# The half-filled sixth tile of the feed-forward: its down product in two passes, with the low part of the activations beside the high part

## The chip, the cores and the metric

The kernel runs on one NeuronCore of a Trainium2 chip. The metric is the device time of one execution in microseconds, as the median of several runs. A profiled execution has a time of its own, and a span from its first to its last instruction.

## What is computed

Eight sequences of 512 tokens with 256 features pass through two layers. Layer 0 is a rotating recurrence with short convolutions and a gated normalisation, then a mixture of experts. Layer 1 is causal attention with 16 heads of 128, then a feed-forward whose weights are looked up in a table of 16 values. All arithmetic of the reference is float32. What matters here is the last block:

```python
def _L1_ffn_ref(x, lut, gate_idx, up_idx, down_idx):   # INTER = 688, HIDDEN = 256
    def _ghost_linear(x, idx, lut):
        w = lut[idx]
        return jnp.einsum('bsh,oh->bso', x, w)
    gate = _ghost_linear(x, gate_idx, lut)
    up = _ghost_linear(x, up_idx, lut)
    h = jax.nn.silu(gate) * up
    return _ghost_linear(h, down_idx, lut)
...
x = x + _L1_ffn_ref(_layernorm(x, axis=-1), L1_ffn_lut, L1_ffn_gate_idx, L1_ffn_up_idx, L1_ffn_down_idx)
```

## The kernel before

**Products in three passes.** Where the reference multiplies float32 matrices, the kernel splits each operand into a high part (the value copied to FP32R, by ScalarE, `high` at L647) and a low part (the value less its high part, by VectorE, `low` at L1055). `mm3` (L1621 to L1623) adds up three matmuls: high times high, high times low, low times high. In the down product the first operand, which sits in the array, is the activation and the second, which streams, is the weight. So L1621 is activation high by weight high, L1622 activation high by weight low, L1623 activation low by weight high. The profile names the two operands of a matmul the other way about: `bank<-fw_high,fa_high` is L1621.

**The feed-forward.** The 688 inner features are laid out in NM = 6 tiles of 128 partitions. Five are full (NFULL = 5). The sixth, m = 5, holds 48 features, padded to 64. Its gate and up rows share one product (`rest`): gate in bank rows 0 to 63, up in rows 64 to 127. ScalarE applies SiLU to the first half, VectorE multiplies it by the second half into `ft` (`ffn_product`, L1506), ScalarE copies the high part into `fa2[0]` (`high_unit`), VectorE writes the low part into `fa2[1]` (`ffn_low`, L1509). `fa2` is a pair of tiles of 128 partitions x 6 x 512 tokens. Rows 64 to 127 of m = 5 hold no features: both parts are cleared there once, ahead of the first batch's low part (two memsets, L1514), and the weights have zeros in the same rows.

**The down product.** For one batch `ffn_down` (L2010) is called for n = 0 and 1. Each call does two of the four token tiles of 128; a token tile is 6 x 3 matmuls that add up in half a PSUM bank, 128 tokens x 256 features. The last batch uses `last_down` (L2019), which goes by m and does all four token tiles for each.

**Where it stands in the order of work.** Each engine's program is written out by hand and in order. Layer 1's attention is a loop over 8 batches x 16 heads (g = 16 b + h). TensorE's share of one head (`head`, in the tensor block) is: `extra_read` and `project_out` of the head before, `make_qk` of the next, `transpose_probs`, `make_v` of the one after next, then `extra`, then `make_z`, then `scores` of the next head. `extra` holds the work of the feed-forward of the batch before: at heads 6 to 11 the gate and up products (H_UNIT = 6), at heads 13 and 14 the two `ffn_down` calls (H_DOWN = 13). The down product of batch 6 and all of batch 7's feed-forward follow behind the last head. VectorE's `head` has `score_max`, `low_q`, `low_probs`, `low_k`, then `ffn_low`, then the rest down to `low_z`; `project_out` on TensorE waits for `low_z`. At head 12 VectorE also writes the low part of the next batch's normalised input (`h_low`).

**Weights.** The host sends table indices `fidx`, which the kernel turns into weights early on; `down` is a view of 128 partitions x 6 x 256 of the weights' high and low tiles. Indices that pad are LUTN = 16, which gives zero.

**Other matmuls that are spoken of.** The output projection of layer 0 (`out_product`, L1699 and L1703, and `out_product_part`, L1716 and L1720) is in float32. For a pair of sequences it first uses 128 rows of partitions (L1699, L1716), then 64 rows, partitions 0 to 63 or 64 to 127 (L1703, L1720). `rows_product` makes layer 0's projections in three passes; of 192 rows of weights it takes 128 and then 64, as 128 and 64 columns of the array.

Of the kernel before, what the change touches and what calls it, by code (L numbers as in the profile page):

```python
# [17 lines left out]
ALU = mybir.AluOpType  # L18
ACT = mybir.ActivationFunctionType
F32 = mybir.dt.float32  # L20
# [5 lines left out]
P = 128  # L26
NB, T, D = 8, 512, 256
# [19 lines left out]
NFULL = INTER // P  # L47
REST = INTER - NFULL * P
NM = NFULL + 1
# [48 lines left out]
def two_layer_program(nc, x_in, w0, wab, cw, invf, rmsw, wo0, cent, gbias, wexp, iota16, tri, tileno, wpair, fidx, lut, out):  # L98
    ctx = ExitStack()
    with ctx:  # L100
        def sb(name, shape, dt=F32):
            return ctx.enter_context(nc.sbuf_tensor(name, shape, dt))

        def sem(name):
            return ctx.enter_context(nc.semaphore(name))
# [4 lines left out]
        bank = [ctx.enter_context(nc.psum_tensor(f"bank{i}", [P, 512], F32)) for i in range(8)]  # L110
# [76 lines left out]
        fa2 = [sb(f"fa2_{part}", [P, NM, T], F32R) for part in ("high", "low")]  # L187
# [37 lines left out]
        ft = [sb(f"ft{i}", [P, T]) for i in range(2)]  # L225
# [6 lines left out]
        def ffn_weights(part):  # L232
            w = fw2[part]
            at = [0, KD * NFULL * P, 2 * KD * NFULL * P, KD * (2 * NFULL + 1) * P, FW]
            views = [w[:, a:b] for a, b in zip(at, at[1:])]
            return [view.rearrange("p (k n) -> p k n", k=KD) for view in views[:3]] + [
                views[3].rearrange("p (m n) -> p m n", m=NM)]
# [126 lines left out]
        s_fa = sem("ffn_activation_split")  # L364
# [44 lines left out]
        def down_bank(b):  # L409
            return {LAST_BATCH: 4, LAST_BATCH - 1: 2}.get(b, 6)  # L410
# [612 lines left out]
        def _(v):  # L1023
# [27 lines left out]
            def low(parts, src, done, at=lambda part: part[:], scale=None):  # L1051

                high_ = at(parts[0]).bitcast(F32)
                if scale is None:
                    v.tensor_tensor(at(parts[1]), src, high_, ALU.subtract).then_inc(done, 1)  # L1055
                else:
                    v.scalar_tensor_tensor(at(parts[1]), src, scale, high_, ALU.mult, ALU.subtract).then_inc(done, 1)
# [450 lines left out]

            def ffn_low(b, m):  # L1509
                v.wait_ge(s_fh, b * NM + m + 1)  # L1510
                used = slice(0, P if m < NFULL else P // 2)
                if b == 0 and m == NFULL:
                    for part in fa2:
                        v.memset(part[P // 2:P, m, :].bitcast(F32), 0.0)  # L1514
                low(fa2, ft[m % 2][used, :], s_fa, lambda part: part[used, m, :])

            def ffn_add(b, n):
                v.wait_ge(s_fd, 2 * b + n + 1)
# [3 lines left out]
            def head(g):  # L1522
# [25 lines left out]
                if b > 0 and H_UNIT < h <= H_UNIT + NM:  # L1548
                    ffn_low(b - 1, h - H_UNIT - 1)
# [29 lines left out]
            for i in range(NT):  # L1579
# [4 lines left out]
                ins = v.bn_stats(stats[:, i, :], xs[0][:, i, :])  # L1584
# [20 lines left out]
            for m in range(NM):  # L1605
                if m + 1 < NM:
                    ffn_product(last, m + 1)
                ffn_low(last, m)
# [4 lines left out]
        def _(pe):  # L1613
            mm = pe.matmul
# [4 lines left out]
            def mm3(dst, w, x, start, stop):  # L1619

                mm(dst, w[0], x[0], start=start, stop=False)  # L1621
                mm(dst, w[0], x[1], start=False, stop=False)  # L1622
                return mm(dst, w[1], x[0], start=False, stop=stop)  # L1623

            def parts(pair, at):
                return [at(t) for t in pair]

            def project3(dst, w_at, x):

                for k in range(KD):  # L1630
                    ins = mm3(dst, [w_at(part, k) for part in range(2)], parts(x, lambda t: t[:, k, :]),
                              k == 0, k == KD - 1)
                return ins
# [362 lines left out]
            gate, up, rest, down = zip(ffn_weights(0), ffn_weights(1))  # L1996

            def ffn_unit(b, m):
# [8 lines left out]
                project3(bank[n][:], lambda part, k: gate[part][:, k, m * P:(m + 1) * P], f2).then_inc(s_fg, 1)  # L2007
                project3(bank[n + 1][:], lambda part, k: up[part][:, k, m * P:(m + 1) * P], f2).then_inc(s_fu, 1)

            def ffn_down(b, n):  # L2010
                pe.wait_ge(s_fa, (b + 1) * NM)
                for i in (2 * n, 2 * n + 1):
                    for m in range(NM):
                        ins = mm3(bank[down_bank(b) + n][:, (i % 2) * D:(i % 2 + 1) * D],
                                  parts(fa2, lambda t: t[:, m, i * P:(i + 1) * P]), [w[:, m, :] for w in down],
                                  m == 0, m == NM - 1)
                ins.then_inc(s_fd, 1)

            def last_down(m):  # L2019
                b = LAST_BATCH  # L2020
                pe.wait_ge(s_fa, b * NM + m + 1)
                for i in range(NT):
                    ins = mm3(bank[down_bank(b) + i // 2][:, (i % 2) * D:(i % 2 + 1) * D],
                              parts(fa2, lambda t: t[:, m, i * P:(i + 1) * P]), [w[:, m, :] for w in down],
                              m == 0 and i % 2 == 0, m == NM - 1 and i % 2 == 1)
                    if m == NM - 1 and i % 2 == 1:
                        ins.then_inc(s_fd, 1)

            def extra(g):
                b, h = divmod(g, NH)  # L2030
                if b > 0:
                    if h == H_TURN3:
                        pe.wait_ge(s_ob, g + START)
                        turn(3, b - 1)
                    if 0 <= h - H_UNIT < NM:
                        pe.wait_ge(s_ob, g + START)
                        ffn_unit(b - 1, h - H_UNIT)
                    if b < LAST_BATCH and 0 <= h - H_DOWN < 2:
                        pe.wait_ge(s_ob, g + START)
                        ffn_down(b - 1, h - H_DOWN)  # L2040
                if b + 1 < NB and h == H_TURN2:
                    pe.wait_ge(s_ob, g + START)
                    turn(2, b + 1)
# [40 lines left out]
            for n in range(2):  # L2084
                ffn_down(last - 1, n)
            pe.wait_ge(s_ob, NG + START)
            turn(3, last)
            for m in range(NM):
                if m >= 2:
                    pe.wait_ge(s_fm, last * NM + m - 1)  # L2090
                ffn_unit(last, m)
                if m >= 2:
                    last_down(m - 2)
            for m in (NM - 2, NM - 1):
                last_down(m)
# [76 lines left out]
```

## Time and profile before

| | us |
|---|---|
| median of three runs | 2242.14 |
| lowest, highest | 2241.34, 2242.36 |
| profiled execution, its own time | 2239.54 |
| its span, first to last instruction | 2237.8 |
| TensorE busy in the span | 2142.9 (96%) |
| VectorE busy | 1678.7 (75%) |
| ScalarE busy | 1375.3 (61%) |
| GpSimd busy | 539.9 (24%) |

PE is TensorE's matmuls, PEld its weight loads, which can run beneath matmuls; DVE is VectorE, ACT ScalarE, POOL GpSimd. Matmuls are pipelined and the end of one is modelled, so their durations overlap: what a matmul costs is the distance from its start to the next one's start. A form such as `64*128` at a matmul is rows times columns of the array in use. "issue" in place of a releaser means that the engine waited for nothing that the profile shows.

### The profile page before, as it was taken

Reading aid. Unit: us, or ns where it says so; the run is one execution under the profiler, and the core shown is the slowest. Engines: PE = TensorE matmul, PEld = TensorE weight load, DVE = VectorE, ACT = ScalarE, POOL = GpSimd, SP = SyncE. Lnnn points to the kernel's source line nnn. Section 1 sums busy time; section 2 is a strip of 40 time slices with the busy share of each in tenths; the row PEclk is TensorE's granted clock in tenths of the full one; section 3 lists DMA queues with packets and bytes.
Section 4 is the critical chain, followed back from the end, with each engine's and each line's share of the span. In section 5 each row is a group of like instructions: output and inputs, shape, how many; then the busy total and the mean of one; then the engine's idle time right before and its main releaser. Section 6 shows DMA issues by size and latency. Waiting matters only on the chain. (4 is left out here: it accounts for less than half of the span.)

```text
span 2237.8 us, 37588 instructions
## 1 busy us (share of the span) xinstructions
PE 2142.9 (96%) x13012; PEld 1862.8 (83%) x13012; DVE 1678.7 (75%) x4385; ACT 1375.3 (61%) x3554; POOL 539.9 (24%) x522
## 2 busy tenths in 40 slices
PE   6899999869999999999999999999999999999998
PEld 5677777747788899889989998998898899899887
DVE  7888897888875777876866777677677768767664
ACT  4443433125636766785786678578677757866772
POOL 0212323420113323222321321231141222122220
PEclk9999999999999999999999999999999999999999
DMA  8001000236531112111211211121121121111100
GB/s 293 1 1 53 24 34 24 101 136 206 174 118 38 62 53 67 57 43 62 67 43 39 89 44 39 62 71 39 39 90 43 39 81 53 38 44 61 39 20 20
DMA packets 88555, 145.81 MB, mean 65 GB/s; under 512 B 8368, under 2 KB 55856, under 8 KB 88368
## 3 DMA queue, kind: packets, MB, share of 16 engines
q1 hardware_dynamic: 67904, 112.73, 15.7%
q0 software_dynamic: 6144, 16.79, 2.2%
q10 hardware_dynamic: 14320, 13.90, 1.8%
q8 instruction: 106, 1.74, 0.3%
q14 instruction: 81, 0.66, 0.1%
HBM read 105.63 MB, written 37.75 MB: 64 GB/s over the span
## 5 line engine op out<-in xcount | busy, mean ns | idle before, releaser
L602 POOL TENSOR_TENSOR wo_low<-wraw_o,wo_high 128x256 fp32r<-128x256 f32 x128 | 94.5, 739 | 1097.5 <-ACT wo_high L647 1097.5
L939 ACT ACTIVATE pr<-bank,negmax 128x128 f32<-128x128 f32 (+3 forms) x512 | 263.0, 526 | 143.7 <-DVE negmax L1465 143.7
L1055 DVE TENSOR_TENSOR p_low<-bank,p_high 128x512 fp32r<-128x512 f32 (+2 forms) x384 | 190.4, 551 | 116.0 <-ACT p_high L647 115.4
L647 ACT ACTIVATE p_high<-bank 128x512 fp32r<-128x512 f32 (+2 forms) x384 | 177.8, 497 | 150.0 <-PE bank L1967 150.0
L1465 DVE CUSTOM_DVE_ANT_0 bank<-bank,causal 128x128 f32<-128x128 f32 (+3 forms) x512 | 234.9, 521 | 1.1 <-PE bank L1623 1.1
L1492 DVE SCALAR_TENSOR_TENSOR xs<-bank,rinv,xs 128x256 f32<-128x256 f32 x512 | 211.9, 477 | 1.2 <-PE bank L1623 1.2
L1621 PE MATMUL bank<-h_high,wqk_high 128*128 128x512 f32 x512 | 203.4, 397 | 2.2 <-DVE h_low L1055 2.2
L1622 PE MATMUL bank<-h_low,wqk_high 128*128 128x512 f32 x512 | 203.4, 397 | 0.0
L1623 PE MATMUL bank<-h_high,wqk_low 128*128 128x512 f32 x512 | 203.3, 397 | 0.0
L592 POOL TENSOR_TENSOR wqk_low<-wraw,wqk_high 128x512 fp32r<-128x512 f32 x128 | 165.5, 1293 | 81.5 <-ACT wqk_high L647 81.5
L1055 DVE TENSOR_TENSOR z_low<-bank,z_high 128x512 fp32r<-128x512 f32 x128 | 88.5, 691 | 128.0 <-ACT z_high L647 127.9
L1967 PEld LDWEIGHTS bank<-ident,pr 128*128 128x128 f32 x1280 | 147.7, 140 | 18.6 <-ACT pr L939 1.4
L1967 PE MATMUL bank<-ident,pr 128*128 128x128 f32 x1280 | 160.5, 272 | 1.1 <-ACT pr L939 1.1
L1621 PE MATMUL bank<-wo_high,z_high 128*128 128x256 f32 x512 | 148.2, 289 | 9.2 <-DVE z_low L1055 6.5
L1621 PE MATMUL bank<-wv_high,h_high 128*128 128x256 f32 x512 | 154.9, 303 | 0.0
L1623 PE MATMUL bank<-wv_high,h_low 128*128 128x256 f32 x512 | 144.5, 282 | 0.0
L1622 PE MATMUL bank<-wv_low,h_high 128*128 128x256 f32 x512 | 144.3, 282 | 0.0
L1622 PE MATMUL bank<-wo_low,z_high 128*128 128x256 f32 x512 | 144.2, 282 | 0.0
L1623 PE MATMUL bank<-wo_high,z_low 128*128 128x256 f32 x512 | 144.1, 281 | 0.0
L1621 PE MATMUL bank<-k_high,q_high 128*128 128x384 f32 (+2 forms) x384 | 140.8, 367 | 0.0
L1621 PE MATMUL bank<-p_high,v_high 128*128 128x512 f32 (+2 forms) x384 | 130.8, 341 | 1.7 <-DVE p_low L1055 1.7
L647 ACT ACTIVATE z_high<-bank 128x512 fp32r<-128x512 f32 x128 | 76.4, 597 | 88.9 <-PE bank L1978 88.9
(312 smaller groups left out, 6436.1 us busy)
## 6 DMA issues: line engine op xcount, KB each, us to landing
wraw<-in_wpair SPq DMA_DIRECT2D x64, 512.0 KB, 4.1
wraw<-in_wpair SPq DMA_DIRECT2D x64, 256.0 KB, 4.3
wraw_o<-in_wpair SPq DMA_DIRECT2D x64, 256.0 KB, 2.5
tokens_by_expert<-zero SPq DMA_DIRECT2D x10, 1024.0 KB, 10.5
xt<-tokens_by_expert SPq DMA_DIRECT2D x40, 256.0 KB, 3.2
expert_results<-ey ACTq DMA_DIRECT2D x40, 256.0 KB, 3.6
wres<-in_wexp SPq DMA_DIRECT2D x1, 6144.0 KB, 20.7
xs<-x_between_stages SPq DMA_DIRECT2D x8, 512.0 KB, 4.6
```

The lines of the kernel that those rows point to most:

```text
L592: pool.tensor_tensor(low, wraw[r][:, 2 * e * D:2 * (e + 1) * D], high.bitcast(F32), ALU.subtract).then_inc(s_wq, 1)
L602: pool.tensor_tensor(wo2[e][1][:], wraw_o[r][:, e, :], wo2[e][0][:].bitcast(F32), ALU.subtract).then_inc(s_wo, 1)
L647: sc.activation(dst, src, ACT.Copy, scale=scale).then_inc(done, 1)
L939: ins = sc.activation(pr[:, i, 0:(i + 1) * P], score(i), ACT.Exp, scale=-1.0, bias=negmax[:, i:i + 1], accum_out=rsum[:, i:i + 1])
L1055: v.tensor_tensor(at(parts[1]), src, high_, ALU.subtract).then_inc(done, 1)
L1465: ins = v.tensor_tensor_reduce(score(i), score(i), causal[:, (NT - 1 - i) * P:NT * P], -1.0, -NEG, ALU.add, ALU.min, negmax[:, i:i + 1])
L1492: ins = v.scalar_tensor_tensor(xb[:, i, :], bank[6 + n][:, (i % 2) * D:(i % 2 + 1) * D], rinv[:, i:i + 1], xb[:, i, :], ALU.mult, ALU.add)
L1621: mm(dst, w[0], x[0], start=start, stop=False)
L1622: mm(dst, w[0], x[1], start=False, stop=False)
L1623: return mm(dst, w[1], x[0], start=False, stop=stop)
L1967: ins = pe.transpose(bank[2 + n][:, at:at + P], pr[:, i, j * P:(j + 1) * P], ident[:])
```

## The change

Rows 64 to 127 of the sixth tile are put to use. `ffn_low` for m = 5 writes the low part of the activations to rows 64 to 127 of the high tile `fa2[0]`, below the high part in rows 0 to 63, and the two memsets go. On the host the sixth tile of the down weights' rows is laid out twice, in rows 0 to 63 and again in rows 64 to 127. The new `down_product` keeps three matmuls for full tiles. For m = 5 it has two: all 128 rows of `fa2[0]` by the high weights, which adds high times high and low times high at once, and rows 0 to 63 of `fa2[0]` by rows 0 to 63 of the low weights. Both `ffn_down` and `last_down` use it. Waits and semaphores stay.

```diff
--- before.py
+++ after.py
@@ -1508,11 +1508,12 @@
 
             def ffn_low(b, m):
                 v.wait_ge(s_fh, b * NM + m + 1)
-                used = slice(0, P if m < NFULL else P // 2)
-                if b == 0 and m == NFULL:
-                    for part in fa2:
-                        v.memset(part[P // 2:P, m, :].bitcast(F32), 0.0)
-                low(fa2, ft[m % 2][used, :], s_fa, lambda part: part[used, m, :])
+                used = slice(0, P // 2)
+                if m < NFULL:
+                    low(fa2, ft[m % 2][:], s_fa, lambda part: part[:, m, :])
+                else:
+                    v.tensor_tensor(fa2[0][P // 2:P, m, :], ft[m % 2][used, :], fa2[0][used, m, :].bitcast(F32),
+                                    ALU.subtract).then_inc(s_fa, 1)
 
             def ffn_add(b, n):
                 v.wait_ge(s_fd, 2 * b + n + 1)
@@ -2007,22 +2008,28 @@
                 project3(bank[n][:], lambda part, k: gate[part][:, k, m * P:(m + 1) * P], f2).then_inc(s_fg, 1)
                 project3(bank[n + 1][:], lambda part, k: up[part][:, k, m * P:(m + 1) * P], f2).then_inc(s_fu, 1)
 
+            def down_product(dst, m, i, start, stop):
+                at = slice(i * P, (i + 1) * P)
+                if m < NFULL:
+                    return mm3(dst, parts(fa2, lambda t: t[:, m, at]), [w[:, m, :] for w in down], start, stop)
+                used = slice(0, P // 2)
+                mm(dst, fa2[0][:, m, at], down[0][:, m, :], start=start, stop=False)
+                return mm(dst, fa2[0][used, m, at], down[1][used, m, :], start=False, stop=stop)
+
             def ffn_down(b, n):
                 pe.wait_ge(s_fa, (b + 1) * NM)
                 for i in (2 * n, 2 * n + 1):
                     for m in range(NM):
-                        ins = mm3(bank[down_bank(b) + n][:, (i % 2) * D:(i % 2 + 1) * D],
-                                  parts(fa2, lambda t: t[:, m, i * P:(i + 1) * P]), [w[:, m, :] for w in down],
-                                  m == 0, m == NM - 1)
+                        ins = down_product(bank[down_bank(b) + n][:, (i % 2) * D:(i % 2 + 1) * D], m, i,
+                                           m == 0, m == NM - 1)
                 ins.then_inc(s_fd, 1)
 
             def last_down(m):
                 b = LAST_BATCH
                 pe.wait_ge(s_fa, b * NM + m + 1)
                 for i in range(NT):
-                    ins = mm3(bank[down_bank(b) + i // 2][:, (i % 2) * D:(i % 2 + 1) * D],
-                              parts(fa2, lambda t: t[:, m, i * P:(i + 1) * P]), [w[:, m, :] for w in down],
-                              m == 0 and i % 2 == 0, m == NM - 1 and i % 2 == 1)
+                    ins = down_product(bank[down_bank(b) + i // 2][:, (i % 2) * D:(i % 2 + 1) * D], m, i,
+                                       m == 0 and i % 2 == 0, m == NM - 1 and i % 2 == 1)
                     if m == NM - 1 and i % 2 == 1:
                         ins.then_inc(s_fd, 1)
 
@@ -2151,8 +2158,10 @@
 
     full = slice(0, NFULL * P)
     rest = np.concatenate([padded(idx[NFULL * P:], P // 2) for idx in (gi, ui)])
+    down_rest = padded(di.T[full.stop:], P // 2)
+    down_rows = np.concatenate([di.T[full], down_rest, down_rest])
     fidx = np.concatenate([kt(gi[full].T).reshape(P, -1), kt(ui[full].T).reshape(P, -1), kt(rest.T).reshape(P, -1),
-                           padded(di.T, NM * P).reshape(NM, P, D).transpose(1, 0, 2).reshape(P, -1)], 1)
+                           down_rows.reshape(NM, P, D).transpose(1, 0, 2).reshape(P, -1)], 1)
     fidx = fidx.reshape(P, NB, LC).transpose(1, 0, 2)
     lut = np.tile(a["L1_ffn_lut"], (P, 1))
 
```

## Rows read from the trace of the kernel before

**Rows 1.** The page: busy us, share, instructions; granted clock in 40 slices.

```profile
PE 2142.9 (96%) x13012; PEld 1862.8 (83%) x13012; DVE 1678.7 (75%) x4385; ACT 1375.3 (61%) x3554; POOL 539.9 (24%) x522
...
PEclk9999999999999999999999999999999999999999
```

**Rows 2.** Waits of TensorE, 890 to 2195 us: total us, times, longest.

```profile
PE bank L1621 <- DVE z_low L1055: 6.5, 8, 0.9
PE bank L1621 <- DVE p_low L1055: 1.7, 2, 0.8
PE bank L1621 <- issue: 1.5, 1, 1.5
PE bank L1967 <- ACT pr L939: 1.1, 1, 1.1
```

**Rows 3.** Groups by form, down product: count, busy us, mean ns, idle before.

```profile
L1621 PE MATMUL bank<-fw_high,fa_high 128*128 128x256 f32 x192 | 54.4, 283 | 0.6 <-DVE fa_low L1055 0.6
...
L1621 PEld LDWEIGHTS bank<-fw_high,fa_high 128*128 128x128 f32 x192 | 36.7, 191 | 0.9 <-DVE fa_low L1055 0.8
```

**Rows 4.** Timeline of PE, end of a down product: start, us, instruction.

```profile
1018.91 0.28 PE L1622 MATMUL bank<-fw_low,fa_high 128*128 128x256 f32 x1
1019.03 0.28 PE L1623 MATMUL bank<-fw_high,fa_low 128*128 128x256 f32 x1
1019.15 0.40 PE L1621 MATMUL bank<-p_high,v_high 128*128 128x512 f32 x1
```

**Rows 5.** Timeline of PE, layer 0's output projection, 359 to 364 us.

```profile
359.13 0.59 PE L1699 MATMUL bank<-wo_all,go 128*128 128x256 f32 x2
359.66 0.70 PE L1703 MATMUL bank<-wo_rest,ge 64*128 64x256 f32 x2
360.19 0.59 PE L1703 MATMUL bank<-wo_rest,go 64*128 64x256 f32 x2
...
362.78 0.59 PE L1703 MATMUL bank<-wo_rest,go 64*128 64x256 f32 x2
363.30 0.50 PE L1621 MATMUL bank<-hT_high,w_high 128*128 128x512 f32 x1
363.64 0.39 PE L1622 MATMUL bank<-hT_low,w_high 128*128 128x512 f32 x1
```

**Rows 6.** Waits of the weight loads, whole span: total us, times, longest.

```profile
PEld bank L1703 <- issue: 2.0, 6, 0.3
...
PEld bank L1720 <- issue: 1.0, 3, 0.3
```

**Rows 7.** Timeline of PE in `rows_product`, from 128 to 64 columns.

```profile
307.65 0.39 PE L1623 MATMUL bank<-hT_high,w_low 128*128 128x512 f32 x1
307.88 0.40 PE L1621 MATMUL bank<-hT_high,w_high 128*64 128x512 f32 x1
308.12 0.39 PE L1622 MATMUL bank<-hT_low,w_high 128*64 128x512 f32 x1
```

**Rows 8.** Timeline of all engines, batch 1, head 12, 1001 to 1008.5 us.

```profile
1002.71 0.69 DVE L1055 TENSOR_TENSOR k_low<-bank,k_high 128x512 fp32r<-128x512 f32 x1
...
1003.56 0.48 DVE L1514 MEMSET fa_high<- 64x512 f32 x1 [0.16 <-issue]
1004.11 0.48 DVE L1514 MEMSET fa_low<- 64x512 f32 x1
...
1008.01 0.36 PE L1621 MATMUL bank<-wo_high,z_high 128*128 128x256 f32 x1 [0.87 <-DVE z_low L1055]
```

**Rows 9.** Timeline of all engines, batch 2, head 12, 1196.5 to 1202 us.

```profile
1196.72 0.69 DVE L1055 TENSOR_TENSOR k_low<-bank,k_high 128x512 fp32r<-128x512 f32 x1
...
1201.12 0.35 PE L1621 MATMUL bank<-wo_high,z_high 128*128 128x256 f32 x1
```

**Rows 10.** Groups by form on DVE, sixth tile: product and subtraction.

```profile
L1506 DVE TENSOR_TENSOR ft<-fsg,bank 64x512 f32<-64x512 f32 x8 | 5.5, 690 | 16.7 <-ACT fsg L959 16.7
...
L1055 DVE TENSOR_TENSOR fa_low<-ft,fa_high 64x512 fp32r<-64x512 f32 x8 | 5.4, 676 | 0.1
```

## Prediction

> **What bounds the kernel now.** I read the page first. TensorE is busy for 2142.9 of 2237.8 us and its granted clock stands at nine tenths or more in every slice [rows 1]. Busy alone proves little, since matmuls overlap, so next come the waits of TensorE in the stretch where the feed-forward runs inside the heads, 890 to 2195 us: 6.5 + 1.7 + 1.5 + 1.1 = 10.8 us of waiting in 1305 us [rows 2]. Nothing else holds TensorE there. Any array time added or taken in a head is therefore a change of the span, with no slack of another engine to swallow it. Third, the groups by form: the down product is 192 matmuls at each of its three lines, 576 in all [rows 3] (the other two lines have the same count). A sixth of them, 96, belong to tile m = 5.
>
> The mean of 283 ns in that group is no price. The timeline gives it: successive down matmuls start at 1018.91, 1019.03 and 1019.15, so one costs 0.12 us of the engine's time [rows 4], and the work behind the product, the first of make_z, follows at the same step without a gap.
>
> **The matmuls removed.** For each of 8 batches and 4 token tiles, tile m = 5 goes from three matmuls to two: 32 fewer, 32 x 0.12 = 3.84 us less [rows 4]. The first remaining pass keeps its shape (128 rows). The second has 64 rows and as many columns. How long does a 64-row matmul take? The output projection of layer 0 has some: between 360.19 and 362.78 six pairs of 64-row matmuls go by, 2.59 us for twelve, 0.216 us each, and such a pair lasts 0.59 us like the pair of 128 rows at 359.13, which has as many columns [rows 5]. Half the rows save nothing in time, so the second pass is taken at the full 0.12 us. Bounds: 0.06 if halving the rows halved the time, for which no row speaks, and 0.12.
>
> **The changes of shape that are added.** This is the part that decides. Now every matmul of the down product has 128 rows. Afterwards each token tile of each batch goes 128 rows to 64 and back to 128 rows. The same crossing stands in the trace [rows 5]:
> - In: the last 128-row matmul starts at 359.13 + 0.216 = 359.35. The first 64-row one starts at 359.66, 0.31 later where 0.216 is the step. That pair lasts 0.70 rather than 0.59: its second starts one step before 360.19, at 359.98, 0.32 later where again 0.216 is normal. Cost: 0.09 + 0.11 = 0.20 us.
> - Out: the last 64-row one starts at 362.78 + 0.216 = 363.00, the next 128-row one at 363.30, 0.31 against 0.216, and the one after it at 363.64, 0.34 against the step of 0.23 to 0.24 for 512 columns [rows 5, 7]. Cost: 0.09 + 0.10 to 0.11 = 0.195 us.
>
> The waits of the weight loads say what happens in the gap: ahead of the first 64-row weight load the load path stood idle 0.33 us, for no semaphore ("issue"), 6 times for 2.0 us at one line and 3 times for 1.0 us at the other [rows 6]. That is all nine entries of that product, each alike. So at a crossing the next weights aren't loaded beneath the running matmul; the load begins late and its own time is then exposed. The row behind the crossing out is an FP32R matmul as here; the one ahead of the crossing in is FP32, and no row has an entry out of FP32R. I take the two prices as they stand, because they are fixed times (about 0.1 us of waiting and 0.1 us of loading) and don't look like a share of the 0.216 us matmul.
>
> In the new program there are 32 crossings in, and 31 out (behind the very last product TensorE has nothing left): 32 x 0.197 + 31 x 0.195 = 6.3 + 6.0 = 12.3 us added. Bounds for a crossing: zero, as in the change of the column count in layer 0, where matmuls of 64 columns of weights follow those of 128 with starts at 307.65, 307.88 and 308.12 and no gap [rows 7]; and above, a full wait for the preceding matmul's recorded 0.283 [rows 3] and a fully exposed load. A load's record is 0.191 us [rows 3]; 0.283 + 0.191 + 0.12 against the usual two steps of 0.24 gives 0.35 us. I stay with 0.195 because the shown rows change rows, as the edit does, while the zero is of columns.
>
> The Trainium skill has a rule for this: "Mode switching requires drain: Changing tiling mode (not just tile) drains the TensorE" (TensorEngine Tiling (Array Packing), Key Properties). By it the change pays at each crossing, and the trace's row changes agree with it at about 0.2 us each; but the same section counts 128 rows by 64 columns as another mode too, and at that change the trace shows no cost [rows 7]. Where the two differ the rows stand.
>
> **The two memsets that go.** Once, in batch 1's head 12, VectorE clears the lower halves of the sixth tile. That isn't hidden: from 1003.56 to 1004.60 VectorE does the two, and project_out then waits 0.87 us for z_low [rows 8]. Batch 2's same head has no memset, and from k_low's start to project_out's first matmul it takes 1201.12 - 1196.72 = 4.40 us where batch 1 takes 1008.01 - 1002.71 = 5.30 [rows 8, 9]. The 0.87 is the longest of the eight waits for z_low [rows 2]. So 0.9 us goes. Bounds: 0 and 0.9.
>
> **What costs nothing.** The low part of the sixth tile is written to partitions 64 to 127 of the high tile from inputs on 0 to 63. The instruction keeps its 64x512 shape; the product before it already crosses partitions the same way (bank rows 64 to 127 with inputs on 0 to 63) and takes 690 ns against 676 for the subtraction that doesn't [rows 10]. Eight such instructions at 14 ns more would be 0.1 us on VectorE, and only the last batch's has TensorE waiting behind it: 0.01 us, left out. The wait on s_fa and its counts are unchanged, so nothing new queues behind it on any engine. The weight index table has the same size and row pitch: same DMAs, same decoding on the other engines, other values. No queue is passed by a moved instruction.
>
> **Sum.** 12.3 added, 3.84 and 0.9 taken away: +7.6 us. Against the profiled execution's own time, 2239.54 us (span 2237.8), that is 2247.1. The median of the runs shown, 2242.14, lies 2.6 above that execution, so the time to expect is 2242.14 + 7.6 = 2249.7 us, 0.34% slower.
>
> **Rivals.**
> 1. The other side: TensorE loads the 64-row weights beneath the running matmul, as it does at the change of columns [rows 7]. For it: the moving operand is short, both matmuls are FP32R and read the same tile. Against it: nine entries of nine in [rows 6]. It gives 2242.14 - 3.84 - 0.9 = 2237.4 us, 0.21% faster, just on the line of what can be told. The point from which it decides is the price of an in-and-out pair: under 4.74 / 32 = 0.15 us the change doesn't slow the kernel; the rows show 0.39. A rule of the skill stands on this side, that the queue pulls a weight load ahead when it goes to the background weights (TensorE: Matmul & The Clock Gate, Part 2).
> 2. Only one of the two crossings costs, since the FP32 entry isn't what the FP32R one is: 31 x 0.195 - 3.84 - 0.9 = +1.3, 2243.4 us, no change that can be told. Against it: entry and exit cost the same to 0.01 us in [rows 5] although one leads to FP32 and the other to FP32R.
> 3. Dearer: a full drain and load, 0.35 us at each of 63 crossings, 22.1 - 4.7 = +17.3, 2259.5 us. For it: the second pass adds to the very PSUM cells that the first has just written, whereas in layer 0 the crossing comes with a change of bank. Against it: within one shape such additions follow each other at 0.12 us [rows 4].
> 4. A crossing costs, but TensorE's longer stay in heads 13 and 14 lets VectorE catch up and a wait vanishes. There is no wait behind those heads to vanish [rows 2], so it gets no chance of its own.
>
> **How the numbers follow.** A measurement of this kernel can tell about 0.2%, 4.5 us, from no change. Chances: the forecast 0.75 (its own range 2246.7 to 2253, from crossings of 0.18 to 0.24); rival 1 0.13, split between faster (0.07) and same (0.06) as its time is on the line; rival 2 0.07, same; rival 3 0.05, slower. Faster 0.07, same 0.13, slower 0.80. The range leaves out rivals 1 and 3 (0.18) and reaches from rival 2's 2243 to 2256, half way to rival 3 for crossings dearer than shown.
>
> **What would show it.** In the trace afterwards: 544 down matmuls, 32 of them with 64 rows; ahead of each an idle weight path of about 0.2 to 0.3 us; the next start after it late by 0.1 too, and the same behind it. One token tile then takes 17 x 0.12 + 0.39 = 2.43 us, against 2.16 now. Batch 1's head 12 from k_low to project_out: 4.4 us. The forecast is wrong if the 64-row weight load begins with the matmul ahead of it and the starts stay 0.12 apart (rival 1), or if the gaps are there and the span doesn't grow, which would mean that TensorE isn't what sets the pace of heads 13 and 14.

## The result, and the profile after

The changed kernel takes 2250.1 us against 2242.5 for the kernel before, medians of 14 runs each: a ratio of 1.0035 with a 95% interval of 1.0025 to 1.0045. It is 7.6 us slower, as much as the sum gave (the forecast was 2249.7).

| | before | after |
|---|---|---|
| median, us | 2242.5 | 2250.1 |
| lowest, highest, us | 2241.2, 2250.3 | 2246.69, 2259.15 |
| profiled execution: its own time, span, us | 2239.54, 2237.8 | 2247.61, 2245.8 |

The page of after has TensorE busy as before, with 32 matmuls fewer than in [rows 1] and 10 us more of busy time. The clock is the same but for the ninth slice (449 to 505 us, 8 for 9), far ahead of the changed code. Two lines of the page:

```profile
PE 2152.9 (96%) x12980; PEld 1861.5 (83%) x12980; DVE 1679.1 (75%) x4383; ACT 1376.1 (61%) x3554; POOL 539.3 (24%) x522
...
PEclk9999999989999999999999999999999999999999
```

The groups by form of after, down product alone (mean ns of one, idle time before). Where [rows 3] had 192 matmuls at each of three lines, there are 160 and then 32 and 32. The ones behind a change of rows carry the price in their mean: 293 for 283 at L1622, 379 for the 64-row form. Their weight loads now have idle time, 4.2 us in all ahead of the 32 with 64 rows:

```profile
L1622 PE MATMUL bank<-fw_high,fa_high 128*128 128x256 f32 x160 | 46.8, 293 | 0.6 <-DVE fa_low L1055 0.6
...
L1622 PEld LDWEIGHTS bank<-fw_high,fa_high 128*128 128x128 f32 x160 | 30.4, 190 | 2.8 <-DVE fa_low L1055 0.8
...
L2017 PE MATMUL bank<-fw_low,fa_high 64*128 64x256 f32 x32 | 12.1, 379 | 0.0
L2016 PE MATMUL bank<-fw_high,fa_high 128*128 128x256 f32 x32 | 9.2, 289 | 0.0
...
L2017 PEld LDWEIGHTS bank<-fw_low,fa_high 64*128 64x128 f32 x32 | 5.8, 183 | 4.2
```

The timeline of PE in after, around the end of one token tile (start, us):

```profile
1017.83 0.28 PE L1624 MATMUL bank<-fw_high,fa_low 128*128 128x256 f32 x1
1017.95 0.28 PE L2016 MATMUL bank<-fw_high,fa_high 128*128 128x256 f32 x1
1018.16 0.38 PE L2017 MATMUL bank<-fw_low,fa_high 64*128 64x256 f32 x1
1018.47 0.38 PE L1622 MATMUL bank<-fw_high,fa_high 128*128 128x256 f32 x1
1018.69 0.28 PE L1623 MATMUL bank<-fw_low,fa_high 128*128 128x256 f32 x1
1018.81 0.28 PE L1624 MATMUL bank<-fw_high,fa_low 128*128 128x256 f32 x1
```

The starts lie 0.12, 0.21, 0.31, 0.22 and 0.12 us apart. Three steps that would take 0.36 take 0.74: the visit to 64 rows costs 0.38 us, one side 0.19. The weight loads of the same place:

```profile
1017.83 0.19 PEld L2016 LDWEIGHTS bank<-fw_high,fa_high 128*128 128x128 f32 x1
1018.15 0.18 PEld L2017 LDWEIGHTS bank<-fw_low,fa_high 64*128 64x128 f32 x1
1018.46 0.19 PEld L1622 LDWEIGHTS bank<-fw_high,fa_high 128*128 128x128 f32 x1
```

A load of the usual kind starts with the matmul ahead of its own, 0.12 us early: L2016's at 1017.83 for its matmul at 1017.95. The one for 64 rows should start at 1017.95 and starts at 1018.15, 0.20 late; the next, again for 128 rows, starts with its own matmul and not one ahead. The late load is the first half of the price (0.09 of each side), the load that then runs uncovered the second (0.10).

At batch 1's head 12, where [rows 8] had the memsets, after has (timeline of all engines):

```profile
1004.92 0.69 DVE L1055 TENSOR_TENSOR k_low<-bank,k_high 128x512 fp32r<-128x512 f32 x1
1005.64 0.68 DVE L1515 TENSOR_TENSOR fa_high<-ft,fa_high 64x512 fp32r<-64x512 f32 x1
...
1009.32 0.36 PE L1622 MATMUL bank<-wo_high,z_high 128*128 128x256 f32 x1
```

That is 4.40 us from k_low to project_out's first matmul, as in [rows 9], and one wait for z_low is gone from the eight of [rows 2] (waits of TensorE, after, 890 to 2200 us):

```profile
PE bank L1622 <- DVE z_low L1055: 5.6, 7, 0.8
```

To see the rate at which the two kernels part, take the first matmul of one and the same project_out in batch 2 and in batch 7. Between them lie five batches, 20 token tiles of the down product, and nothing else that was changed. Timelines of PE, first of before, then of after:

```profile
1189.67 0.35 PE L1621 MATMUL bank<-wo_high,z_high 128*128 128x256 f32 x1 [0.81 <-DVE z_low L1055]
...
2155.59 0.35 PE L1621 MATMUL bank<-wo_high,z_high 128*128 128x256 f32 x1 [0.81 <-DVE z_low L1055]
```

```profile
1192.11 0.36 PE L1622 MATMUL bank<-wo_high,z_high 128*128 128x256 f32 x1 [0.78 <-DVE z_low L1055]
...
2163.43 0.36 PE L1622 MATMUL bank<-wo_high,z_high 128*128 128x256 f32 x1 [0.81 <-DVE z_low L1055]
```

965.92 us before, 971.32 after: 5.40 more, 0.27 per token tile. This stretch serves below for every kernel, since it is the steadiest: one that shares its order of work with before came out 0.25 us from it.

The two spans differ by 8.0 us, of which some has nothing to do with the change. At k_low of batch 1's head 12, ahead of every changed instruction, after is already 2.2 us later (1004.92 against 1002.71). And before lost time at its end to a lower clock, after didn't. The stretch 2205 to 2236 us, with TensorE's granted clock as the last but two of the numbers:

```profile
2205.00:2236.00 31.00, 26.81 (x148) 23.06 (x146) 11.69 (x18) 9.18 (x15) 0.00 (x0) 0.94 0.07 24
```

```profile
2205.00:2236.00 31.00, 28.99 (x172) 25.13 (x171) 13.94 (x40) 7.43 (x12) 0.00 (x0) 1.00 0.05 18
```

The first is before, 0.94; the second after, 1.00. Behind a wait of 2.01 us for f_low both kernels start the last batch's products; in before eight steps between matmuls of 512 columns were then made at 1.2 GHz (granted clock 0.52 from 2209.5 to 2213 us), 0.43 us each instead of 0.23 (2209.52 to 2212.91 us), 1.6 us in all. So 2.2 - 0.9 - 1.6 + 32 x 0.26 = 8.0, as the spans have it.

### The profile page after: what moved, and what is told of

It is laid out like the page before. It is cut to its first block and busy times, and to the rows that moved or that the text cites. A ratio compares the mean times of both kernels' runs of the same rounds, so it can differ in the third digit from the quotient of the medians.

```text
span 2245.8 us, 37522 instructions
## 1 busy us (share of the span) xinstructions
PE 2152.9 (96%) x12980; PEld 1861.5 (83%) x12980; DVE 1679.1 (75%) x4383; ACT 1376.1 (61%) x3554; POOL 539.3 (24%) x522
## 5 line engine op out<-in xcount | busy, mean ns | idle before, releaser
L1622 PE MATMUL bank<-h_high,wqk_high 128*128 128x512 f32 x512 | 203.1, 397 | 2.2 <-DVE h_low L1055 2.2
L1622 PE MATMUL bank<-wo_high,z_high 128*128 128x256 f32 x512 | 148.2, 289 | 8.3 <-DVE z_low L1055 5.6
L1622 PE MATMUL bank<-wv_high,h_high 128*128 128x256 f32 x512 | 154.9, 302 | 0.0
L1622 PE MATMUL bank<-k_high,q_high 128*128 128x384 f32 (+2 forms) x384 | 140.9, 367 | 0.0
L1622 PE MATMUL bank<-p_high,v_high 128*128 128x512 f32 (+2 forms) x384 | 132.2, 344 | 1.7 <-DVE p_low L1055 1.7
```

## The experiments

The theory: TensorE pays about 0.19 us whenever successive matmuls change between 128 and 64 rows, because the next weights aren't loaded beneath the running matmul. The rivals: A, the price belongs to two passes from the same activations into the same PSUM cells; B, it belongs to each 64-row matmul; C, any change of the array's shape pays, columns too.

**Two full passes.** The changed kernel with its second pass over 128 rows:

```diff
-                used = slice(0, P // 2)
                 mm(dst, fa2[0][:, m, at], down[0][:, m, :], start=start, stop=False)
-                return mm(dst, fa2[0][used, m, at], down[1][used, m, :], start=False, stop=stop)
+                return mm(dst, fa2[0][:, m, at], down[1][:, m, :], start=False, stop=stop)
```

> The changed kernel with its second pass over all 128 rows of the high tile and of the low weights (it adds low by low, a term that the changed kernel doesn't have). Theory (each change between 128 and 64 rows costs TensorE about 0.19 us): no crossing is left, 544 matmuls at 0.12 us, so 3.84 us and the memsets' 0.9 go: 4.7 us under the kernel before, a ratio of 0.998. Rival A (the price comes from two passes that load weights from the same activations or add to the same PSUM cells): the gaps of 0.21 and 0.31 us stay and the time is that of the changed kernel, 1.0035. Rival B (the 64-row matmul itself is slow, 0.5 us each): as the theory here.

Measured: 2236.59 us against 2243.21, ratio 0.9969, interval 0.9954 to 0.9984. The timeline of PE in this kernel:

```profile
1028.03 0.28 PE L1624 MATMUL bank<-fw_high,fa_low 128*128 128x256 f32 x1
1028.14 0.28 PE L2015 MATMUL bank<-fw_high,fa_high 128*128 128x256 f32 x1
1028.27 0.28 PE L2016 MATMUL bank<-fw_low,fa_high 128*128 128x256 f32 x1
1028.38 0.28 PE L1622 MATMUL bank<-fw_high,fa_high 128*128 128x256 f32 x1
```

The starts are 0.11 to 0.13 us apart throughout, in the same order, from the same activations into the same cells. The stretch of 20 token tiles takes 963.42 us, 2.50 less than before, 0.125 a tile: one matmul. Rival A falls. The measured gain of 6.6 us between medians is more than the 4.7 expected, but the interval (3.6 to 10.3 us) holds the 4.7. This kernel is faster than both: the idea of the change pays when both passes have 128 rows.

**Three short passes.** The kernel before with m = 5 on 64 rows in all three passes, so without its memsets:

```diff
+            def down_product(dst, m, i, start, stop):
+                used = slice(0, P if m < NFULL else P // 2)
+                return mm3(dst, parts(fa2, lambda t: t[used, m, i * P:(i + 1) * P]),
+                           [w[used, m, :] for w in down], start, stop)
```

> The kernel before, with the sixth tile's three passes over 64 rows instead of 128, and no memsets. Theory (the crossing costs, 0.19 us a side): 32 in and 32 out as in the changed kernel, but no matmul saved: +12.2 - 0.9 = +11.3 us, ratio 1.005; in the trace 0.12 us between the starts of 64-row matmuls. Rival B (each 64-row matmul costs 0.38 us more): 96 x 0.38 - 0.9 = +35.6 us, ratio 1.016.

Measured: 2251.8 against 2243.21 us, ratio 1.0037, interval 1.0021 to 1.0053; the 1.005 of the theory is in it, the 1.016 of rival B is far out. (The medians differ by 8.6 us where the theory had 11.3; the interval reaches from 4.7 to 11.9.) The timeline of PE:

```profile
1026.22 0.28 PE L1620 MATMUL bank<-fw_high,fa_low 128*128 128x256 f32 x1
1026.43 0.38 PE L1618 MATMUL bank<-fw_high,fa_high 64*128 64x256 f32 x1
1026.65 0.28 PE L1619 MATMUL bank<-fw_low,fa_high 64*128 64x256 f32 x1
1026.77 0.28 PE L1620 MATMUL bank<-fw_high,fa_low 64*128 64x256 f32 x1
1026.98 0.38 PE L1618 MATMUL bank<-fw_high,fa_high 128*128 128x256 f32 x1
1027.20 0.28 PE L1619 MATMUL bank<-fw_low,fa_high 128*128 128x256 f32 x1
```

With three 64-row matmuls in a row the two sides come apart: 0.21 and 0.22 going in, then 0.12 between the second and the third, then 0.21 and 0.22 coming out. Each side is 0.09 + 0.10. A 64-row matmul behind another costs what a 128-row one costs, 0.12 us. The 20 tiles take 973.96 us, 8.04 more than before, 0.40 a tile.

**Short passes together.** The changed kernel with the 64-row passes of a call moved to its end, two side by side (four in the last batch). The diff is shortened: `(...)` stands for the arguments, `short_pass` is the second matmul of m = 5, and `last_down` is changed alike:

```diff
                 for i in (2 * n, 2 * n + 1):
                     for m in range(NM):
-                        ins = down_product(...)
+                        down_product(...)
+                for i in (2 * n, 2 * n + 1):
+                    ins = short_pass(b, i)
                 ins.then_inc(s_fd, 1)
```

> The changed kernel with the 64-row passes of a call of the down product side by side at its end (two token tiles in 14 calls, four in the last batch). Theory: 15 visits to 64 rows instead of 32, 15 x 0.38 = 5.7 us against 3.84 + 0.9 saved: +1.0 us, ratio 1.0005. Rival B (per matmul): +7.6 us as the changed kernel, ratio 1.0034.

Measured: 2244.52 against 2243.21 us, ratio 1.0012, interval 0.9996 to 1.0027. The expected 1.0005 is inside, the 1.0034 of rival B outside. The timeline shows one visit for two tiles:

```profile
1018.69 0.28 PE L2015 MATMUL bank<-fw_high,fa_high 128*128 128x256 f32 x1
1018.90 0.50 PE L2019 MATMUL bank<-fw_low,fa_high 64*128 64x256 f32 x2
1019.33 0.50 PE L1622 MATMUL bank<-p_high,v_high 128*128 128x512 f32 x1
```

In the stretch there are 10 visits and 20 matmuls fewer: 967.48 us, 1.56 more than before, so (1.56 + 20 x 0.12) / 10 = 0.40 us a visit. The number of visits sets the price, not the number of matmuls. Halving the visits is enough to bring the changed kernel so near to before that the comparison can't tell them apart.

**Second pass over 64 columns.** Two full passes, the low weights' pass first and only for 64 of a tile's 128 tokens:

```diff
-                mm(dst, fa2[0][:, m, at], down[0][:, m, :], start=start, stop=False)
-                return mm(dst, fa2[0][:, m, at], down[1][:, m, :], start=False, stop=stop)
+                half = slice(i * P, i * P + P // 2)
+                mm(dst[0:P // 2, :], fa2[0][:, m, half], down[1][:, m, :], start=start, stop=False)
+                return mm(dst, fa2[0][:, m, at], down[0][:, m, :], start=False, stop=stop)
```

> Both passes over 128 rows, the shorter one first and only for the first 64 tokens of each token tile (64 columns of the array, output rows 0 to 63): high by low is left out for the other 64 tokens in the sixth tile. Theory (a change of columns costs nothing, as in layer 0): starts stay 0.12 us apart, the end of the span like two full passes, about 4.7 us under the kernel before. Rival C (any change of the array's shape drains it, as the Trainium skill's TensorEngine Tiling page has it in Key Properties): gaps of 0.21 and 0.31 us at each of the 32 visits and the changed kernel's time, +7.6 us.

One run: 2241.48 us, which alone says little; the timeline of PE decides:

```profile
1022.61 0.28 PE L1624 MATMUL bank<-fw_high,fa_low 128*128 128x256 f32 x1
1022.72 0.28 PE L2016 MATMUL bank<-fw_low,fa_high 128*64 128x256 f32 x1
1022.84 0.28 PE L2017 MATMUL bank<-fw_high,fa_high 128*128 128x256 f32 x1
1022.96 0.28 PE L1622 MATMUL bank<-fw_high,fa_high 128*128 128x256 f32 x1
```

128 by 64 and back with no gap at either side; the 20 tiles take 963.13 us, 2.79 less than before, like two full passes. Rival C falls: this change of columns is free, at the very place where rows cost 0.38 us. The Trainium skill (TensorEngine Tiling (Array Packing), Available Configurations and Key Properties) lists both 64×128 and 128×64 as modes and has a drain at every change of mode. For rows the runs agree with a price. For columns they show none; the profile gives the columns in use and not the mode, so whether the array was in the 128×64 mode of the Trainium skill isn't shown.

**Memsets in head 7.** The kernel before, with its memsets five heads earlier:

```diff
-                if b == 0 and m == NFULL:
+                if b == 0 and m == 0:
                     for part in fa2:
-                        v.memset(part[P // 2:P, m, :].bitcast(F32), 0.0)
+                        v.memset(part[P // 2:P, NFULL, :].bitcast(F32), 0.0)
```

> The kernel before with its two memsets five heads earlier, in front of the first tile's low part of the first batch. Theory (at head 12 they delay z_low because VectorE also writes the next batch's low part there): batch 1's head 12 takes 4.4 us from k_low to the first matmul of project_out instead of 5.3 and its wait for z_low goes, while the earlier head swallows the 1.0 us: TensorE waits for z_low 7 times, and 0.9 us goes. Rival (the wait of 0.87 us is only moved along with the memsets): a wait for z_low of about that size at head 7.

One run: 2241.79 us. In the trace (timeline of all engines, batch 1's head 12) the first matmul of project_out comes 1011.51 - 1007.11 = 4.40 us after k_low, and the waits of TensorE between 690 and 2198 us have seven for z_low, where before has eight. The first two lines are project_out's first matmuls on either side of the memsets' new place (942.55 to 943.57 us):

```profile
934.66 0.33 PE L1621 MATMUL bank<-wo_high,z_high 128*128 128x256 f32 x1
...
947.81 0.33 PE L1621 MATMUL bank<-wo_high,z_high 128*128 128x256 f32 x1
...
1007.11 0.69 DVE L1055 TENSOR_TENSOR k_low<-bank,k_high 128x512 fp32r<-128x512 f32 x1
...
1011.51 0.36 PE L1621 MATMUL bank<-wo_high,z_high 128*128 128x256 f32 x1
```

```profile
PE bank L1621 <- DVE z_low L1055: 5.8, 7, 0.8
```

The wait didn't come back at head 7: the step from one project_out to the next is 13.15 us across the memsets, and the same step in before, without them, is 13.15 too (930.34 to 943.49). So the memsets alone cost 0.9 us, by their place.

**Layer 0 with 128 rows.** Two full passes, and the crossings of layer 0 taken away too; each sequence's output projection then holds a part of the other's:

```diff
-                        ins = mm(dst(i), src[half, SPLIT_ROW, i * P:(i + 1) * P], wo_rest[half, par, :], start=False,
+                        ins = mm(dst(i), src[:, SPLIT_ROW, i * P:(i + 1) * P], wo_rest[:, par, :], start=False,
```

> Two full passes in the sixth tile and, in layer 0's output projection, 128 rows where 64 are used: it adds the other sequence's product to each, so layer 0's output is another. Theory (the price belongs to any change of the row count, FP32 or FP32R): the idle times of 0.33 us before L1703 and L1720 go, and no weight load of these lines waits; up to 9 x 0.39 = 3.5 us less of TensorE's time in layer 0, of which the span gets only what other engines don't wait for, 0 to 3.5 us beyond two full passes, so 4.7 to 8.2 us under the kernel before. Rival (the gap there belongs to the change of PSUM bank): the gaps stay.

Measured: 2236.61 against 2243.8 us, ratio 0.9963, interval 0.9949 to 0.9978, which can't be told from two full passes alone (0.9969). Locally the price goes. Where [rows 5] had 0.53 us for each of the two steps around the crossing, the timeline of PE has 0.43, as between any two pairs, and no weight load of L1704 or L1721 waits:

```profile
357.99 0.59 PE L1700 MATMUL bank<-wo_all,go 128*128 128x256 f32 x2
358.42 0.59 PE L1704 MATMUL bank<-wo_rest,ge 128*128 128x256 f32 x2
358.85 0.59 PE L1704 MATMUL bank<-wo_rest,go 128*128 128x256 f32 x2
```

The PSUM bank changes there as before, so the bank isn't the cause. The 0.4 us a visit, up to 3.5 us in all, is smaller than this comparison can show, and how much of it the span gets was not settled.

## Why the prediction was right, point by point

The terms of the sum were right one by one, as the points below have it. That the medians differ by 7.6 us, just as the sum had it, is luck to that accuracy: the interval reaches from 5.6 to 10.1 us. The firm evidence is the 0.27 us per token tile.

- *TensorE sets the pace, with no slack to swallow anything.* Right: 0.27 us more for each of 20 token tiles in the steady stretch, where the sum has 0.39 - 0.12 = 0.27.
- *A matmul of the down product costs 0.12 us, 32 of them go.* Right: two full passes gave 0.125 a tile.
- *A 64-row matmul takes as long as a 128-row one.* Right: 0.12 us between two of them in three short passes.
- *A crossing costs 0.197 in and 0.195 out, by layer 0's rows.* Right to 0.01: 0.19 each in the changed kernel. The step that was open, whether an entry from FP32R costs what one from FP32 does, went the way of the FP32 row. The entry costs 0.21 + 0.22 - 0.24 = 0.19 us in the down product (three short passes) and 0.20 in layer 0; at one clock it is a fixed time, as was assumed, since a matmul's step is 0.12 us in the one and 0.216 in the other. So rival 2 fell (both sides cost), rival 3 had the wrong size, and rival 1 the wrong mechanism: at this change the load doesn't start beneath the running matmul (1018.15 where 1017.95 would be usual).
- *The memsets cost 0.9 us.* Right, shown by moving them alone. Without that term the sum would have been 8.5.
- *The bound of zero from the change of columns.* It was a true row of another thing: columns are free at the down product too. It made the range wider than the rows of the same change did.
- *The write across partitions costs nothing.* Right: the eight subtractions at L1515 take 685 ns each where [rows 10] had 676.
- *The forecast's own range*, 2246.7 to 2253, was said to come from crossings of 0.18 to 0.24 us. 63 of those less 4.74 give 2248.7 to 2252.5; nothing in the working gives its lower end.
- One remark was wrong and cost nothing: behind the last batch's sixth tile TensorE was said to wait for the low part. The wait of 0.58 us stands ahead of the fifth tile's product, and the sixth tile's follows at once.
- *The marks.* A token tile takes 1020.88 - 1018.47 = 2.41 us from start to start where 2.43 was given. The idle time of the weight path ahead of a late load was given as 0.2 to 0.3 us, from FP32 rows, and is 0.13 (1017.83 + 0.19 to 1018.15): what is 0.20 us is the lateness.

## What to carry to other kernels

Count changes of the row count, not matmuls: in these traces one side costs 0.19 us, so a detour through 64 rows must save more than three matmuls of 256 columns, and filling the unused rows, with zeros as before did or with the low by low term as two full passes did, was cheaper. Where short passes are needed, put them side by side; a change between 128 and 64 columns can be left where it is. Small one-off instructions on an engine that is 75% busy aren't free by that number: two memsets cost 0.9 us in one head and nothing five heads earlier.

## What the runs showed of the hardware that was not expected

**Rows pay and columns don't**, 0.38 us against nothing a visit, at the same place of the down product. Only 128 and 64 were tried.

**A lower clock at the end of layer 0.** The profiled execution of two full passes took 2247.24 us, where the median of that kernel is 2236.59. Its stretch at the end of layer 0 and that of short passes together (PE alone; the granted clock is again the last but two of the numbers):

```profile
438.00:456.00 18.00, 16.94 (x64) 0.72 0.78 294
```

```profile
438.00:456.00 18.00, 18.00 (x94) 1.00 0.87 329
```

In both, TensorE had waited 2.30 us for ScalarE's rexp, worked, and waited 1.06 us for sq. The first from 442.8 on ran at 1.2 GHz for about ten microseconds (granted clock 0.52 from 442.8 to 453 us), with pairs of 1.06 us for 0.59, which by estimate costs about five; the second kept 2.4 GHz. That code is the same in both. What decides was not found. Such a drop can make up a part of the scatter of one kernel's executions, not all of it: the profiled execution of three short passes took 2260.57 us against a median of 2251.8 and had a granted clock of 1.00 from 437 to 475 us. That is why differences of 3 to 8 us were read from a stretch of layer 1 and not from single spans. At the lower clock a crossing costs more, but not double (timeline of PE in that execution):

```profile
442.83 1.06 PE L1717 MATMUL bank<-wo_all,go 128*128 128x256 f32 x2
443.82 1.22 PE L1721 MATMUL bank<-wo_rest,ge 64*128 64x256 f32 x2
444.84 1.05 PE L1721 MATMUL bank<-wo_rest,go 64*128 64x256 f32 x2
```

Steps within a shape are 0.427 us there. The second of the first pair starts at 443.26 and the 64-row one 0.56 later, its second at 444.84 - 0.43 = 444.41, 0.59 later: together 2.01 us from 442.83 to 444.84 where four steps take 1.71, so 0.30 us for this one entry where 2.4 GHz has 0.20.
